# The filing stage of a graph layer, taken two tiles at a time instead of one

## The reference, cut to what matters

```
xn  = layernorm(x)
agg = segment_sum(xn[src], dst) / max(degree, 1)          # and again with dst, src exchanged
h   = relu(xn @ W0_0 + b0_0 + agg @ W1_0 + b1_0)          # a second graph convolution follows
x   = x + gnn(xn) + linear_attention(xn)
x   = x + top2_of_8_experts(layernorm(x))
```

## Time and profile before

| what | value |
|---|---|
| time, median of 3 runs | 2232.6 us (2228.12 to 2233.89) |
| the profiled execution | 2227.12 us, its span 2225.2 us |
| busy, share of the span | PE 93%, DVE 69%, ACT 54%, POOL 17% |
| instructions | PE 15356 matmuls, DVE 4838, ACT 2515 |
| filing: one-hots of tile 0 to those of tile 48 | 33.3 to 307.1 us from the span's start |

### The profile page before, as it was taken

The page is one execution under the profiler, slowest core; times in us unless marked ns, Lnnn a source line. Parts: engine busy times, 40 slices in busy tenths (PEclk is TensorE's granted clock), DMA queues, the critical chain, the costliest instruction groups (busy, mean ns, idle before and its releaser), DMA issues.

```text
span 2225.2 us, 52275 instructions
## 1 busy us (share of the span) xinstructions
PE 2067.5 (93%) x15356; PEld 1305.8 (59%) x15357; DVE 1544.1 (69%) x4838; ACT 1210.1 (54%) x2515; POOL 367.8 (17%) x434
## 2 busy tenths in 40 slices
PE   3888889999999999999999998999999995999996
PEld 2676675555555555555554543444444443899996
DVE  6998977999999999998555544455444544455554
ACT  4777754555555555555656543444444443666664
POOL 2000000000000000000111111111222112466665
PEclk9999998999999999999999999999999997999998
DMA  3333246222222222223444336555555555555552
GB/s 95 93 95 92 89 126 190 113 109 116 116 117 116 109 117 116 112 112 128 167 144 147 119 120 219 199 198 197 193 194 194 195 212 177 129 94 93 88 94 42
DMA packets 158734, 299.11 MB, mean 134 GB/s; under 512 B 31774, under 2 KB 107855, under 8 KB 156419
## 3 DMA queue, kind: packets, MB, share of 16 engines
q1 hardware_dynamic: 131075, 243.66, 31.6%
q0 software_dynamic: 25856, 47.15, 9.4%
q10 hardware_dynamic: 1664, 6.35, 0.8%
HBM read 148.32 MB, written 144.19 MB: 131 GB/s over the span
## 4 chain that ended last, share of the span: by engine, by line
PE 68%; issue 13%; DVE 9%; DVEq 4%; DMA 2%; POOL 1%; ACT 1%; POOLq 1%; ACTq 0%; SPq 0%
PE bank L2280 44%; PE bank L2271 6%; PE bank L2519 6%; PE bank L2504 6%; DVE big L1132 1%; DVE big L1145 1%; DVE big L1127 1%; PE bank L2486 1%; DVEq L1141 1%; PE bank L2288 1%; POOLq L843 1%; DVE big L1143 1%; DMA rows_dram<-big 1%; DVEq L1129 1%; DMA big<-rows_dram 1%
## 5 line engine op out<-in xcount | busy, mean ns | idle before, releaser
L2280 PE MATMUL bank<-RW,big 128*128 128x512 f16 x4753 | 1148.3, 380 | 0.0
L2280 PEld LDWEIGHTS bank<-RW,big 128*128 128x128 f16 x4753 | 431.3, 98 | 384.5 <-issue 3.2
L1929 ACT ACTIVATE big<-bank 128x512 f16<-128x512 f32 (+1 forms) x640 | 364.2, 573 | 316.1 <-PE bank L2271 316.1
L1301 DVE TENSOR_TENSOR big<-iotaB,keys 128x512 f16<-128x512 f16 x1300 | 452.4, 420 | 8.0 <-issue 6.8
L2271 PEld LDWEIGHTS bank<-big 128*128 128x128 f16 x2560 | 190.8, 98 | 106.3 <-DVE big L1301 1.5
L2271 PE MATMUL bank<-big 128*128 128x128 f16 x2560 | 247.2, 219 | 0.8 <-DVE big L1301 0.8
L986 POOL DMA_INDIRECT out_dram<-big x112 | 179.8, 1605 | 109.9 <-ACT big L2074 75.5
L910 POOL DMA_DIRECT2D big<-in_L_ffn_W_dram x8 | 6.2, 777 | 1041.3 <-DVE R L1360 1040.6
L2065 ACT ACTIVATE big<-bank,b1A,iscA 128x256 f32<-128x256 f32 x224 | 114.0, 559 | 99.0 <-PE bank L2504 88.5
L2504 PE MATMUL bank<-big,RW 128*128 128x256 f16 x1344 | 157.3, 274 | 0.4 <-ACT big L2054 0.4
L2519 PE MATMUL bank<-RW,big 128*128 (+1 forms) x1344 | 156.9, 274 | 0.2 <-DVE big L1724 0.2
(11 more groups left out here) (422 smaller groups left out, 2919.2 us busy)
## 6 DMA issues: line engine op xcount, KB each, us to landing
big<-a_dram SPq DMA_DIRECT2D x48, 800.0 KB, 6.0
big<-a_dram SPq DMA_DIRECT2D x48, 768.0 KB, 4.2
a_dram<-big SPq DMA_DIRECT2D x49, 640.0 KB, 3.0
a_dram<-big SPq DMA_DIRECT2D x49, 512.0 KB, 2.6
a_dram<-big SPq DMA_DIRECT2D x49, 416.0 KB, 2.4
big<-rows_dram SPq DMA_DIRECT2D x56, 265.0 KB
big<-in_x_dram SPq DMA_DIRECT2D x96, 128.0 KB, 2.1
own_dram<-big SPq DMA_DIRECT2D x48, 256.0 KB, 2.5
```

The lines of the kernel that those rows point to most:

```text
L1301: last = v.tensor_tensor(out[q].rearrange("p b (m k) -> p b m k", k=2), inturn(iotaB[:, :], QB, P // 2), twice(kd[:, q * QB:(q + 1) * QB, ...
L1929: a.activation(Ab[q][:, 0:n], banks[BB(q)][:, 0:n], ACT.Copy).then_inc(s_ab, 1)
L2280: last = mm(bank[:, :], blk(q, c), R2[:, u * 2 * D:(u + 1) * 2 * D], start=(i == 0), stop=(i == T - 1))
```

## The change

VectorE's work on OH, V, the base product, the fold, the sum and R1 is done for two tiles in one instruction: 38 x 52 and 38 x 80 elements in place of 19 x 52 and 19 x 80. There are 25 steps p, the last with one tile. OH, V, R1 and base become two buffers of two tiles; the base product is written over OH. `values` is a function of its own now and stands behind `inverse`. One reciprocal serves two tiles. ScalarE and TensorE still work by single tiles, but take those of a pair together: base1 and table1 twice in every second step, before1 and file1 likewise. The core of the diff:

```
+            def onehots(p):
+                n, sl = pair(p)
+                if p >= 2:
+                    dve.wait_ge(s_before, 2 * p - 2)
+                v.tensor_tensor(OH[p % 2][:, 0:n * U].rearrange("p (c m k) -> p c m k", c=n, k=2),
+                                inturn(iotaU[:, :], n, U // 2), twice(key2[:, sl, :], n, U // 2),
                                 ALU.is_equal).then_inc(s_oh, 1)
                 dve.drain()
...
+            def ranks(p):
+                n, sl = pair(p)
+                a = n // CAP
+                oh = OH[p % 2][:, 0:n * U]
+                dve.wait_ge(s_base, 2 * p + a)
...
-            def inverse(t):
-                i = t % 2
-                dve.wait_ge(s_std, t + 1)
-                if t >= 2:
-                    dve.wait_ge(s_xn, t - 1)
-                v.reciprocal(rstd[:, i:i + 1], sums[:, i, 3:4]).then_inc(s_stat, 1)
+            def inverse(p):
+                n = min(2, T - 2 * p)
+                dve.wait_ge(s_std, 2 * p + n)
+                if p:
+                    dve.wait_ge(s_xn, 2 * p)
+                v.reciprocal(rstd[:, 0:n], sums[:, 0:n, 3]).then_inc(s_stat, n)
...
+            onehots(0)
+            values(0)
+            for p in range(PAIRS):
+                if p + 1 < PAIRS:
+                    onehots(p + 1)
+                ranks(p)
+                if p + 1 < PAIRS:
+                    inverse(p + 1)
+                    values(p + 1)
+                for t in range(2 * p, min(2 * p + 2, T)):
```

Here n is 38 columns (19 for the last, single tile) and a the number of tiles. Behind these, inside the loop over t, stand the pieces for the next group, now at t % 7 = 0, 1, 2 and 3 (they were at 2 to 5), and decode, at 1 as before. On ScalarE:

```
+            base1(1)
             for t in range(T):
                 normal1(t)
-                if t + 1 < T:
-                    base1(t + 1)
-                if t:
-                    table1(t - 1)
+                if t % 2 == 0:
+                    for i in range(t + 2, min(t + 4, T)):
+                        base1(i)
+                    for i in range(max(t - 2, 0), t):
+                        table1(i)
                 if t >= 3:
                     own1(t - 3)
                 if t + 2 < T:
                     deviation1(t + 2)
```

On TensorE, where before1 of both tiles waits for the pair's one-hots:

```
+                pe.wait_ge(s_oh, t // 2 + 1)
...
+                if t % 2 == 0:
+                    for i in range(t + 2, min(t + 4, T)):
+                        before1(i, i % 2)
                 gram(t)
                 if t >= 2:
                     own1(t - 2)
-                file1(t, t % 2)
+                if t % 2 or t == T - 1:
+                    for i in range(t // 2 * 2, t + 1):
+                        file1(i, i % 2)
```

More of the change, by code:

```diff
@@ L262, in gps_layer @@
         sp1 = Space()
-        OH = [sp1.f16(CAP * U) for _ in range(2)]
-        V = [sp1.f16(CAP * U) for _ in range(3)]
-        R1 = [sp1.f16(CAP * DEPTH) for _ in range(2)]
+        OH = [sp1.f16(2 * CAP * U) for _ in range(2)]
+        V[0], R1[0] = sp1.f16(2 * CAP * U), sp1.f16(2 * CAP * DEPTH)
         W7 = [sp1.f16(PACK * U) for _ in range(2)]
         wq, wm = (sp1.f16(PACK * U).bitcast(I16) for _ in range(2))
[L268 to L271, removed]
+        base = [sp1.f16(2 * U) for _ in range(2)]
+        held = sp1.f32(2 * CAP)
+        rank2 = sp1.f16(2 * CAP * 2).rearrange("p (c k) -> p c k", k=2)
         A12 = sp1.f16(2 * T * U).rearrange("p (k n) -> p k n", k=2)
@@ L1132, in onehots, with values @@
[L1132 to L1140, removed]
-                dve.drain()
-                pv = prod.rearrange("p (c u) -> p c u", u=U)
+            def values(p):
+                n, sl = pair(p)
+                if p >= 2:
+                    dve.wait_ge(s_filed, 2 * p - 2)
+                v.tensor_tensor(V[p % 2][:, 0:n * U].rearrange("p (c m k) -> p c m k", c=n, k=2),
+                                OH[p % 2][:, 0:n * U].rearrange("p (c m k) -> p c m k", c=n, k=2),
+                                twice(ends[:, sl, :], n, U // 2), ALU.mult).then_inc(s_val, 1)
+                dve.drain()
@@ new lines, in ranks @@
+            def ranks(p):
+                n, sl = pair(p)
+                a = n // CAP
+                oh = OH[p % 2][:, 0:n * U]
+                dve.wait_ge(s_base, 2 * p + a)
+                v.tensor_tensor(oh.rearrange("p (a c u) -> p a c u", a=a, u=U), oh.rearrange("p (a c u) -> p a c u", a=a, u=U),
+                                base[p % 2][:, 0:a * U].rearrange("p (a c u) -> p a c u", a=a, c=1)
+                                .to_broadcast([P, a, CAP, U]), ALU.mult)
+                dve.drain()
+                pv = oh.rearrange("p (c u) -> p c u", u=U)
@@ L1219, in _ @@
             within1(0)
-            onehots(0, 0)
-            for t in range(T):
-                g, i = t // PACK + 1, t % PACK
-                if t + 1 < T:
[L1224 to L1252, removed]
-                    last.then_inc(s_wpl, 1)
@@ new lines, in _ @@
+            onehots(0)
[8 more added lines that the diff above has]
+                for t in range(2 * p, min(2 * p + 2, T)):
+                    g, i = t // PACK + 1, t % PACK
+                    if g < NG:
+                        if i == 0:
+                            words1(g)
+                        if i == 1:
+                            keys1(g)
+                        if i == 2:
+                            same1(g)
+                        if i == 3:
+                            within1(g)
+                    if i == 1 and t > PACK:
+                        decode(t // PACK - 1)
+                    if t == 12:
+                        dve.wait_ge(s_w, 16 * 16)
+                        v.tensor_tensor(bhs[:, :], bh[:, 0, :], bh[:, 1, :], ALU.add).then_inc(s_bh, 1)
+                    if t == 28:
+                        dve.wait_ge(s_sp, 1)
+                        v.tensor_reduce(small[:, 35:39], banks[4][:, 0:8].rearrange("p (a k) -> p a k", k=2), AX.X, ALU.add)
+                        v.tensor_copy(small[:, 39:40], banks[4][:, 8:9]).then_inc(s_sp, 1)
+                    if t == 34:
+                        scales1()
+                    if t == 38:
+                        dve.wait_ge(s_wph, 1)
+                        for k in range(2):
+                            last = v.scalar_tensor_tensor(out=W1T[1][:, k, :], in0=W1s[:, k, :], scalar=wsc,
+                                                          in1=W1T[0][:, k, :], op0=ALU.mult, op1=ALU.subtract)
+                        last.then_inc(s_wpl, 1)
```

60 lines of the change are left out of this document (28 added, 32 removed).

## The result

The changed kernel takes **2303.83 us** (median of three runs, 2300.38 to 2304.29) against 2233.01 us for the kernel before on the same chip: **1.0317 times as long, 95% interval 1.0295 to 1.0339**, 71 us slower. (A fourth run of it took 2981.9 us at a granted TensorE clock of 0.69, where the other three had 0.96, and is left out; with it the median is 2304.06 us.) The profiled execution took 2300.38 us, with a span of 2298.8 us, against 2227.12 and 2225.2.

What follows compares the result with a forecast made beforehand. VectorE set the pace before; the change makes it wait in a closed circle. 23 rounds of 11.33 us, group work 56.4 and smaller terms end filing 51 us later: 2232.6 + 51 = 2284 us, 8-in-10 range 2262 to 2308.

Steps and rivals of the forecast that it cites:

- Merged instructions: VectorE in the filing stage: 7.82 us for a pair against 9.06 for two tiles, 30 us of work saved.
- The rival of a lost fast rate: VectorE's merged one-hots and values cost twice as much per element: 49 us more, 2333 us; chance 0.03.
- The closed pass: Filing loop: one-hots, count, base copy, two deviations, reciprocal, one-hots close in one round; VectorE waits 3.2 us at the reciprocal.
- The round: Filing loop, one pair: 10.93 us + G in place of 9.06 + G; taken as 11.33 with TensorE's clock.
- fast counts: TensorE's counts without the idle slowdown: two take 1.27 us; all fast gives 42 us lost, all slow 58.
- ScalarE's extra instructions: ScalarE's even steps, between base copies and second deviation: group instructions once hidden by VectorE's pace now add 5.5 us.
- TensorE's clock: After idling, TensorE counts at 1.2 GHz: two slow counts add 0.70 us to a round, 0.40 taken on average.
- The second rival: TensorE at the lower clock throughout the filing stage: another 52 us, 2336 us; chance 0.05.
- The sum: Filing stage: 23 rounds of 11.33, plus G, plus 5.5, less 0.5; last one-hots end at 359.0, 51 us later.
- G: VectorE's group work and other pieces between tiles: 56.4 us in all, 2.35 for each of 24 pairs.
- about the same length: Last ranks, file and decode behind the last one-hots: no difference taken, give or take 2 us.
- The faster rival: VectorE stays the bound, its reciprocal not waiting: 7.82 us + G for a pair, 2203 to 2211 us; chance 0.07.

Runs made afterwards that it cites:

- open ring: The changed kernel with ScalarE's base copies moved behind the pair's deviations and TensorE's counts behind gram and own1: 2226.06 us, ratio 0.9974.
- with drains: The open ring with eight drain instructions added on VectorE ahead of the first reciprocal: 2219.79 us, ratio 0.9942.
- spread open ring: The open ring with the group's pieces spread, about one in each pair and none in the first: 2213.88 us, ratio 0.9917; with eight drains 2209.25 us.

## Why the prediction was right, and by how much it was short

The forecast of 2284 us had the sign and the mechanism; the loss was 71 us where it said 51. The measured time lies inside the range given for 8 in 10 (2262 to 2308), but 8 us above the forecast's own (2270 to 2296), because terms outside the round were sized too small. Point by point:

- **Merged instructions: right.** One-hots to base product 1.27 us (forecast 1.26), base product to fold 1.26 (1.25), fold to sum 0.75 (0.75), sum to place 1.26 (1.26), place to R1 0.31 (0.31), R1 1.74 long, in the timeline above. The rival of a lost fast rate is dead.
- **The closed pass: right, and shown by undoing it** at VectorE (62 us back) and at ScalarE with TensorE (76 us). The wait at the reciprocal was forecast at 74 to 90 us in all and was 85.4; VectorE's busy share at about 70% and was 69%.
- **The round: right to 0.05 us.** From one-hots to reciprocal the sum was 1.17 + 8.43 = 9.60 us with fast counts and 10.30 with slow ones. A round with fast counts, in VectorE's timeline:

```profile
241.96 1.19 DVE L1130 TENSOR_TENSOR big<-iotaU,R 128x1976 f16<-128x1976 f16 x1
...
251.55 0.17 DVE L1185 RECIPROCAL rstd<-sums 128x2 f32<-128x2 f32 x1 [2.99 <-ACT sums L1836]
```

  That is 9.59; rounds with slow counts take 10.25, and the one shown in full 10.90, with one of ScalarE's extra instructions (0.60) in it. Over 23 rounds these stretches sum to 237.2 us; 23 times 10.0, plus 5.5 for the extras, is 235.5.
- **TensorE's clock: right.** The round shown in full, in three short windows:

```profile
157.00:159.00 2.00, 1.97 (x40) 1.97 (x41) 1.86 (x2) 0.32 (x2) 0.00 (x0) 0.50 0.00 0
159.00:162.00 3.00, 3.00 (x11) 2.35 (x10) 2.78 (x4) 2.66 (x11) 0.00 (x0) 0.50 0.01 3
164.00:166.60 2.60, 2.60 (x17) 2.24 (x15) 0.00 (x0) 2.31 (x9) 0.00 (x0) 1.00 0.62 179
```

  After an idle stretch of 5.16 us the 38 count matmuls run at a granted clock of 0.50 (1.2 GHz) in 1.83 us, and by 164 us it is 1.00 (2.4 GHz) again. The second rival, TensorE slow throughout, fails on the last of these rows.
- **The sum: short by 20 us.** The terms "G 56.4" and "about the same length" behind the last one-hots were mis-sized; the traces, whose spans differ by 73.6 us, place it. Up to the last one-hots the loss is 62.3 and not 51. Of these 11 us, 2.1 lie ahead of the loop (first one-hots at 35.4, not 33.3: the first reciprocal already needs two deviations); 4.8 are one wait of `words1` for its DMA (the L1075 row above), because the change calls it at t = 0, when the window of edges that it reads has not arrived (I had counted the moved pieces at their old price and not asked what each waits for at its new place); 1.7 are the rounds; and some 2.4 are in the main a miscount of G. G was what 48 tiles at 4.53 us leave of 273.8, but the first step holds no ranks. In the kernel before the second one-hots start 1.36 us behind the first (at 33.29):

```profile
34.65 0.67 DVE L1127 TENSOR_TENSOR big<-iotaU,R 128x988 f16<-128x988 f16 x1
```

  With that step and 47 tiles, 59.5 us are left and not 56.4, 0.9 of them a wait for a DMA that isn't in the change's G. The group's instructions did not get longer: start to start, waits apart, they add up to 57.9 us in the kernel before and 58.4 in the changed one. Behind the last one-hots come 3.1 us to the merge, 0.2 to the convolution, 4.5 in the convolution (the digits' row) and 3.5 after it. The 3.1 were read wrongly too: behind the last one-hots still lie the ranks of a whole pair, and the last tile's reciprocal waits 1.6 us (11.8 us from there to the end of the last R1, 8.8 before). The 3.5 are no more than the kernel before shows between two executions (4.0).
- **The faster rival: wrong as a forecast, and its price holds only with more edits than it named.** It said 2203 to 2211 us if the reciprocal did not wait. The open ring, where it hardly waits (11.5 us), takes 2226.06 and with drains 2219.79; only with the pieces spread as well does it come to 2209.25. The open ring's last one-hots start 9 us later than the rival's sum would have them (294.1 against 285, from 33.3 + 273.8 - 30 + 8), and 5.2 of these are the wait of `words1` for its DMA, which the rival left out as the forecast did.

On the rule weighed in the prediction: the Trainium skill (Perfetto Trace Analysis, Optimizing Scalar/DVE Operations) has grouping pay where the engine is saturated and breaking up pay where it holds up others. The runs agree with the first half: the same merged instructions took 0.8% off in the spread open ring, where VectorE was 92% busy, and cost 71 us where it stood 85.4 us at the reciprocal. For the second half they show less: the kernel before, with its instructions broken up into single tiles, is 71 us faster than the change, but edits of order gave the 71 us back with nothing broken up.

What stays open: why drains far ahead take the 0.104 us a pass away, and by what, their number's effect on the loop's place or their presence.

## What to carry to other kernels

Merging two steps into one instruction doesn't only halve a fixed cost; it makes every consumer wait for the second half and takes a round of slack out of each circle of waits, so follow every wait around the engines' orders and sum one pass, start to start, before counting what is saved. When a circle has closed, look for all the places where a stream queues something early that it needs late: here the reciprocal alone, or copies and counts together, and not the copies alone. And a call that moves to an earlier step takes its own waits along, DMA arrivals first.

## What the runs showed of the hardware

A loop in VectorE's stream ran with 0.15 us of idle time a pass at one instruction in eight of the profiled executions and with 0.26 in five, its own code being the same: about 5 us in 2220. The five are the merged kernels without drains, and their convolution stage takes 705.0 to 706.7 us; the eight are those of single tiles and the four with drains, at 700.4 to 701.5 us. Eight idle instructions placed ahead brought the shorter time back in three kernels, 31 in one. In the records of VectorE's own sequencer the extra time stands between the end of the drain ahead of the digits and the register instruction behind it: 0.13 us in the changed kernel, 0.03 before and with drains. Kernels of this size are better compared stage by stage than by their totals alone.

The Trainium skill (Runtime: NRT & Kernel Launch, Instruction fetch mechanics) says that instructions are fetched in blocks and in sequence, and that a taken branch out of the blocks at hand stalls; a loop's cost could then hang on its place. No row here shows a fetch, and the extra time stands 2.4 us ahead of the loop's branch and not right behind it, so this is a candidate and no finding.
